# Graph attention sums: ScalarE copies out the bank of the tile that precedes an item's tile, and TensorE works batch by batch

## The reference

```python
q, k, v = h @ Wq, h @ Wk, h @ Wv                     # [n, 8, 32] each
e = sum(q[dst] * k[src], -1) / sqrt(32)              # a score for each edge and head
a = exp(e - segment_max(e, dst)[dst])
z = segment_sum(a, dst)
agg = segment_sum(v[src] * a / (z[dst] + 1e-9), dst) # one row a node
h = layer_norm(agg @ Wo + h)
```

## Time and profile before

| | us |
|---|---|
| median of 3 runs | 6584.65 (6556.1 to 6599.15) |
| the profiled execution | 6544.67 |
| its span in the trace | 6542.9 |

### The profile page before, as it was taken

How to read it: one execution, slowest core, us unless ns; L and a number is a source line. 1 busy time by engine, 2 the same in 40 slices (tenths; PEclk the granted TensorE clock), 3 DMA queues, 4 the chain that set the end, 5 groups by cost and what they waited for, 6 DMA issues and landing times. The chain is left out here.

```text
span 6542.9 us, 104165 instructions
## 1 busy us (share of the span) xinstructions
PE 4595.6 (70%) x23436; PEld 3457.5 (53%) x23437; DVE 3985.9 (61%) x7269; ACT 1997.0 (31%) x4726; POOL 2832.8 (43%) x2898
## 2 busy tenths in 40 slices
PE   0678888888778888888876949655556555348990
PEld 0555555555565666666656949643334433315660
DVE  4667777777576777777656656796444445722332
ACT  0134444444323444444424323320000000313440
POOL 0066666666106666666600010004777776060116
PEclk9999999999889999999888979887777776559995
DMA  5465555555236666665530020002333333022113
GB/s 93 136 189 164 163 163 171 165 164 167 84 109 189 172 169 169 173 169 167 161 103 16 0 94 6 2 29 76 104 104 103 103 105 86 27 90 80 61 56 118
DMA packets 351851, 736.53 MB, mean 113 GB/s; under 512 B 74621, under 2 KB 192897, under 8 KB 351566
## 3 DMA queue, kind: packets, MB, share of 16 engines
q0 software_dynamic: 189824, 588.23, 31.5%
q1 hardware_dynamic: 161870, 146.69, 7.8%
HBM read 634.25 MB, written 100.43 MB: 112 GB/s over the span
## 5 line engine op out<-in xcount | busy, mean ns | idle before, releaser
L967 POOL DMA_INDIRECT rows_a<-kv_scratch,att_idx x848 | 854.6, 1008 | 1096.0 <-issue 563.9
L728 POOL DMA_INDIRECT rows_a<-k_scratch,sage_sum_idx x832 | 799.7, 961 | 855.9 <-issue 850.0
L1027 ACT ACTIVATE attention_rows_b<-ps x1664 | 649.3, 390 | 1366.2 <-PE ps L1120 1237.9
L967 POOL DMA_INDIRECT rows_c<-kv_scratch,att_idx x816 | 877.4, 1075 | 417.9 <-issue 247.1
L1103 PE MATMUL ps<-attention_rows_b,att_work 128*128 x3328 | 925.4, 408 | 72.4 <-issue 60.3
L1435 PE MATMUL ps<-rows_a 128*128 128x258 f32 x1664 | 614.9, 534 | 467.5 <-DMA rows_a<-k_scratch,sage_sum_idx 309.4
L1435 PEld LDWEIGHTS ps<-rows_a 128*128 128x128 f32 x1664 | 421.7, 265 | 660.5 <-DVE sage_rows_b L1413 417.2
L1118 PE MATMUL ps<-rows_a,att_work 128*128 128x264 f32 x1696 | 572.5, 455 | 211.0 <-ACT attention_rows_b L1027 165.0
L1103 PEld LDWEIGHTS ps<-attention_rows_b,att_work 128*128 128x128 f32 x3328 | 608.4, 201 | 184.7 <-issue 92.1
L1413 DVE TENSOR_TENSOR sage_rows_b<-sage_rows_b,ps 128x258 f32 x832 | 353.1, 424 | 566.0 <-PE ps L1435 370.5
L1118 PE MATMUL ps<-rows_c,att_work 128*128 128x264 f32 x1632 | 540.2, 448 | 147.8 <-ACT attention_rows_b L1027 119.1
(11 more groups left out here) (395 smaller groups left out, 9304.4 us busy)
## 6 DMA issues: line engine op xcount, KB each, us to landing
kv_scratch<-rows_c SPq DMA_DIRECT2D x100, 256.0 KB
rows_a<-kv_scratch,att_idx POOLq DMA_INDIRECT x848, 3.7
slot_in<-rows_c SPq DMA_DIRECT2D x1, 13568.0 KB
rows_a<-slot_in SPq DMA_DIRECT2D x106, 128.0 KB
slot_out<-rows_a POOLq DMA_DIRECT2D x106, 128.0 KB
rows_a<-k_scratch,sage_sum_idx POOLq DMA_INDIRECT x832, 2.8
rows_c<-kv_scratch,att_idx POOLq DMA_INDIRECT x816, 3.7
h_scratch<-rows_a SPq DMA_DIRECT2D x2, 6400.0 KB
```

The source lines that it names most:

```text
L728: pool.indirect_dma_start(ring[:, slot, 0:D], None, table, bass.IndirectOffsetOnAxis(ap=idx[:, slot:slot + 1], axis=0)).then_inc(landed[sl ...
L967: pool.indirect_dma_start(r.halves[h][:, u, 0:KV], None, c.kv_dram[:, :], bass.IndirectOffsetOnAxis(ap=idx[:, slot:slot + 1], axis=0)).the ...
L1027: a.activation(c.rows_b[:, bass.ds(at[u], QW)], c.ps[:, bass.ds(in_bank(c, at[BATCH + u]), QW)], ACT.Copy).then_inc(copied, 1)
```

## The change

The table of places gets a fourth kind, and the three kinds of banks are 1: the bank of the *preceding* tile, 2: the bank of the item's tile, 3: the bank of the next tile. `keep` now copies the bank of the preceding tile, at the offset at which it wrote before; so `rows_b` holds the sum of tile t one place further on, at t+1, and one more copy at the end fetches the last tile. The sum, the clear and the copy of an item thus touch three different banks. `summed` is incremented by each item's sum, not by the clear of a pair. A copy waits for the sums of all earlier items; a clear waits for the copies of all earlier items; a sum waits for no copy. `rescale_sums` waits for the block's sums rather than for its copies. TensorE takes the sums of a batch in one piece: in q=0 and q=1 directly after the distances and ahead of the expansions, in q=2 and q=3 after the expansions. ScalarE takes the scores in q=3 ahead of `keep`.

```diff
-        self.places = sb("places", [1, BATCHES * 3 * BATCH], I32)
+        self.places = sb("places", [1, BATCHES * 4 * BATCH], I32)
...
-                    for k in range(2):
+                    for k in range(3):
                         sp.dma_start(c.room_dram[k].rearrange("(c p) -> p c", p=P), bank_i[:, k]).then_inc(written, 16)
-                sp.wait_ge(written, 96)
+                sp.wait_ge(written, 112)
...
-                for k in range(2):
-                    do(v.tensor_copy(places[:, :, 1 + k], bank_rows[:, k, 0:ITEMS].rearrange("p (b u) -> p b u", u=BATCH)))
+                for k, to in enumerate((2, 3, 1)):
+                    do(v.tensor_copy(places[:, :, to], bank_rows[:, k, 0:ITEMS].rearrange("p (b u) -> p b u", u=BATCH)))
...
                 def edge_hot(b, n):
                     a.wait_ge(s_spread, b + 1)
-                    need(a, summed, 2 * b - 2)
+                    need(a, summed, 4 * b - 4)
...
-                def keep(b, between=None):
+                def keep(b):
                     at = places_of(a, c, b, 0, 2)
-                    for half in range(2):
-                        if half and between is not None:
-                            take_scores(between)
-                        a.wait_ge(summed, 2 * b + half + 1)
-                        for u in (2 * half, 2 * half + 1):
-                            need(a, copied, b * BATCH + u)
-                            a.activation(c.rows_b[:, bass.ds(at[u], QW)], c.ps[:, bass.ds(in_bank(c, at[BATCH + u]), QW)],
-                                         ACT.Copy).then_inc(copied, 1)
+                    for u in range(BATCH):
+                        need(a, summed, b * BATCH + u)
+                        need(a, copied, b * BATCH + u)
+                        a.activation(c.rows_b[:, bass.ds(at[u], QW)], c.ps[:, bass.ds(in_bank(c, at[BATCH + u]), QW)],
+                                     ACT.Copy).then_inc(copied, 1)
...
+                        if q == 3 and within(i, ROUND, k + 1, 0, BLOCKS):
+                            take_scores(blk + 1)
                         if sums:
-                            keep(g, blk + 1 if q == 3 and within(i, ROUND, k + 1, 0, BLOCKS) else None)
+                            keep(g)
...
-                a.wait_ge(copied, ITEMS)
+                a.wait_ge(summed, ITEMS)
+                last = 5 * 512 + NODE_TILES % 3 * 512
+                a.activation(c.rows_b[:, NT * QW:(NT + 1) * QW], c.ps[:, last:last + QW], ACT.Copy).then_inc(copied, 1)
+                a.wait_ge(copied, ITEMS + 1)
...
-                def add_up(i, n, at, half):
+                def add_up(i, n):
                     b = i * RB + n
-                    need(pe, copied, b * 4 + 2 * half)
-                    if half == 0:
-                        pe.wait_ge(s_ready, b + 1)
-                        pe.wait_ge(messages, b + 1)
-                        if n % 4 == 0:
-                            need(pe, rescaled, i * 2 * ROUND + n // 4 * 2)
+                    at = places_of(pe, c, b, 2, 2)
+                    pe.wait_ge(s_ready, b + 1)
+                    pe.wait_ge(messages, b + 1)
+                    if n % 4 == 0:
+                        need(pe, rescaled, i * 2 * ROUND + n // 4 * 2)
                     rows = r.batch(n)
-                    for u in (2 * half, 2 * half + 1):
+                    for u in range(BATCH):
                         pe.matmul(c.ps[:, bass.ds(in_bank(c, at[u]), QW)], r.s[n % 2][:, u, :], rows[:, u, D:SLOT],
-                                  start=False, stop=True, skip_group_check=True)
-                        mm = pe.matmul(c.ps[:, bass.ds(in_bank(c, at[BATCH + u]), 1)], c.zeros[:, :], c.zeros[:, 0:1],
-                                       start=True, stop=True)
-                    mm.then_inc(summed, 1)
+                                  start=False, stop=True, skip_group_check=True).then_inc(summed, 1)
+                        need(pe, copied, b * BATCH + u)
+                        pe.matmul(c.ps[:, bass.ds(in_bank(c, at[BATCH + u]), 1)], c.zeros[:, :], c.zeros[:, 0:1],
+                                  start=True, stop=True)
...
-                        if q != 3:
-                            spread(q)
+                        spread(q)
                         if q == 2:
                             turn_weights(blk)
-                        if sums:
-                            at_sum = places_of(pe, c, i * RB + g, 1, 2)
-                        if ahead:
-                            at_q = places_of(pe, c, i * RB + u, 0, 1)
-                        if q == 2 and ahead:
-                            expand(i, u, at_q, 0)
-                            expand(i, u, at_q, 1)
-                        if sums:
-                            add_up(i, g, at_sum, 0)
+                        if q < 2 and sums:
+                            add_up(i, g)
                         if q == 0:
                             turn_ends(blk)
                         if q == 1:
                             carry_columns(blk)
-                        if q == 2:
-                            spread(3)
+                        if ahead:
+                            at_q = places_of(pe, c, i * RB + u, 0, 1)
+                            expand(i, u, at_q, 0)
                         if q == 3 and within(i, ROUND, k + 1, 0, BLOCKS):
                             turn_scores(blk + 1, k + 1)
-                        if q != 2 and ahead:
-                            expand(i, u, at_q, 0)
-                        if sums:
-                            add_up(i, g, at_sum, 1)
-                        if q != 2 and ahead:
+                        if ahead:
                             expand(i, u, at_q, 1)
+                        if q >= 2:
+                            add_up(i, g)
...
                 def rescale_sums(blk):
                     v.wait_ge(r_ready, blk + 1)
-                    v.wait_ge(copied, blk * BLOCK)
-                    at = in_bank(c, places_of(v, c, blk * 4, 1, 1)[0])
+                    v.wait_ge(summed, blk * BLOCK)
+                    at = in_bank(c, places_of(v, c, blk * 4, 2, 1)[0])
```

More of the change, by code:

```diff
@@ L362, in _ @@
                 do(v.tensor_copy(row_f, c.item_tile[:, :]))
-                places = c.places[:, :].rearrange("p (b k u) -> p b k u", k=3, u=BATCH)
+                places = c.places[:, :].rearrange("p (b k u) -> p b k u", k=4, u=BATCH)
                 do(v.tensor_scalar(places[:, :, 0], row_f[:, 0:ITEMS].rearrange("p (b u) -> p b u", u=BATCH),
                                    float(QW), None, ALU.mult))
-                for k in range(2):
-                    do(v.tensor_copy(places[:, :, 1 + k], bank_rows[:, k, 0:ITEMS].rearrange("p (b u) -> p b u", u=BATCH)))
+                for k, to in enumerate((2, 3, 1)):
+                    do(v.tensor_copy(places[:, :, to], bank_rows[:, k, 0:ITEMS].rearrange("p (b u) -> p b u", u=BATCH)))
                 each = row_f.rearrange("p (b u) -> p u b", u=BATCH)
@@ L906, in places_of @@
 def places_of(eng, c, b, first, kinds):
-    at = c.places[0:1, bass.ds(b * 3 * BATCH + first * BATCH, kinds * BATCH)]
+    at = c.places[0:1, bass.ds(b * 4 * BATCH + first * BATCH, kinds * BATCH)]
     return c.nc.values_load_multi_w_load_instructions(
@@ L1002, in stage @@
                 def stage(g, n):
-                    need(a, summed, 4 * g - 20)
+                    need(a, summed, 8 * g - 40)
                     a.activation(idx[:, n * HALF:(n + 1) * HALF], c.src_idx[:, bass.ds(g * HALF, HALF)],
@@ L1535, in norm @@
                 def norm(g, parity):
-                    sums = c.rows_b[:, bass.ds(g * 2 * SUMW, 2 * SUMW)].rearrange("p (t n) -> p t n", t=2)
+                    sums = c.rows_b[:, SUMW:][:, bass.ds(g * 2 * SUMW, 2 * SUMW)].rearrange("p (t n) -> p t n", t=2)
                     v.wait_ge(turned, g + 1)
```

24 lines of the change are left out of this document (11 added, 13 removed).

## The result

| | before | after |
|---|---|---|
| median of the runs, us | 6591.9 (6556.1 to 6609.92, 4 runs) | 6337.07 (6333.12 to 6339.42, 4 runs) |
| profiled execution, us (its span) | 6544.67 (6542.9) | 6339.42 (6337.8) |
| ratio after/before | | 0.9619, 95% interval 0.9577 to 0.9661 |

The changed kernel is 3.8% faster. Between the medians lie 255 us, between the two profiled spans 205.1.

A forecast was written before the change was run, and what follows sets the result against it. TensorE with its waits was taken to set the pace. Blocks 115, loop's turn -6, tables -6, tail +12, last copy -1 made 114, say 115 us, off the 6584.65 median: 6470 us, range 6350 to 6600.

The forecast's parts named there:

- The banks and waits: Mid-loop blocks: pair waits for copies go, new clear waits just covered; 23.7 us for 24.8, 115 us over 104 blocks.
- The stall at the second clear: TensorE in q=0 and again in q=1: second clear waits for ScalarE's first copy, made behind its tables; 0.65 us each.
- The wait for the messages: TensorE in q=2, before the first sum: grows from 0.48 to 1.36 us, where part of the gain goes.
- The tables: Table of places: a third column of bank numbers adds a scattered write on the path; 6 us.
- eight increments more a block: Each sum carries a semaphore increment, 16 a block for 8: nothing counted; 22 us in all if they serialize.
- The layout: The block laid out phase by phase from earlier trace durations: 23.7 us a block, time 6410 to 6520, chance 0.47.
- the baseline: Median of three timed runs, 6584.65 us, 40 above the profiled run; the same 115 us taken from it.
- The tail: Last two batches of a layer: some five uncovered 1.19 us pair waits go; 12 us, less 1 for the last copy.
- The loop's turn: One block in three: ScalarE's lateness stands whole before the second clear, 2.6 us for 2.43; costs 6 us.
- (a): Rival: cover complete, the two stalls and the reads go; block 22.1 to 22.4 us, time 6335; chance 0.14.
- (b): Rival: nothing gained, the wait moves to the softmax chain; block 24.5 to 25 us, time 6555 to 6620; chance 0.21.
- (c): Rival: lockstep, sum-copy-clear round 0.3 us longer, block 1.2 us longer than before, 6720 us; chance 0.14.

The follow-up runs named there:

- fill: Kernel before plus six matmuls that compute nothing, in q=3 where TensorE waited for a copy: 6530.17 us, ratio 0.9895.
- wrap_fill: Changed kernel plus ten matmuls that compute nothing, before the second clear of q=0 in each third block: 6351.41 us, ratio 0.9713.
- tail_fill: Kernel before plus four matmuls that compute nothing behind each half of the sums, in a layer's last block and two batches only: 6577.51 us, ratio 1.0005.
- copy_first: Changed kernel with ScalarE's first copy ahead of its two tables in q=0 and q=1: 6324.5 us, ratio 0.959.
- copy_reads: Changed kernel with ScalarE's first copy ahead of its tables in q=0 and q=1, and TensorE's reads of places moved ahead: 6328.11 us, ratio 0.9675.
- slow_copy: Changed kernel with a small ScalarE operation and a wait for it ahead of each copy: 6725.73 us, ratio 1.0287.

## Why the prediction was right and where it failed

*The banks and waits: right in mechanism and size.* Mid-loop 23.5 us where 23.7 was laid out, 1.23 us a block less and not 1.1. The stall at the second clear of q=1 was 0.68 for 0.65, that of q=0 0.28: the clear came at t=2.17 for 2.28, but the read ahead of the sums had already made TensorE 0.26 late there. The issue gap of 0.62 us went; 0.26 of waiting for the multiply came in its place. The wait for the messages grew to 0.92 and not to 1.36. Reads on the path: 0.17 to 0.32 us for 0.15. `local_max` lost its wait and gathers stayed hidden. The copies behind two waits each follow at 0.58 us and not at the 0.52 taken, so ScalarE is slower than an item and not faster; over the four copies of a batch no clear of q=2 or q=3 came to wait for it. The tables took 3.8 us more for 6 (the first instruction of VectorE behind them, L795, starts at 92.15 us for 88.38), but the first layer's first turn of the scores stands at 373.5 us for 373.8, so nothing of it is left there. Of the eight increments more a block nothing is to be seen: with one on each sum the pace is 0.563 us, as it was. The rule that the prediction named stands in the Trainium skill on the page "TensorE: Matmul & The Clock Gate", section "The cost: per-tile semaphore tail", not on the page that the prediction gave. By it the pace would be 0.576 on the mean of all items, an estimate; the trace does not agree.

*The step that failed is the clock.* The layout counted idle time at its own length, with every matmul at the durations of the earlier trace rows, as if what TensorE is granted were the same before and after. The mean in the earlier trace rows, 25.9 us a block against 24.8, was ascribed to the turn of ScalarE's loop; the second layer, with 25.42 us a block at clock 0.96 and no turn that is 2.5 us late, was not looked at. There a block of before at full clock takes 24.8 or 24.7 us, and 25.3 where the loop turns (2693.13 to 2718.40, the one such block at clock 1.00). The 44 blocks between the first four and the last three took 27 us more than that. After, the same 44 took 0.6 us more than 23.5 and, at the turns, 24.0. The gain of the second layer is 32 us over 51 times 1.23; 26 to 27 of them are this, which no term of the sum held, and the rest lies in the first and last blocks and was not taken apart. `fill`, `wrap_fill` and the trace of `tail_fill` show the clock at work apart from the change. The Trainium skill, "TensorE: Matmul & The Clock Gate", "A second HAM failure mode: psum-queue depth-cycling", tells of a kernel whose short idles between groups of matmuls, from cycling through PSUM banks, make the clock go to and fro between its levels; these traces agree (1.26 us of idle, then 1.24 us for a matmul pair of 0.71).

*The same error in the baseline.* The prediction took the 40 us by which the median of before lay above the profiled run over to the changed kernel. They did not carry over: after, the four runs lie within 6.3 us of each other, and the profiled one is the longest of them. On three chips the median of before was 6600, 6534 and 6548 us, while `copy_first` on the first and its near kin `copy_reads` on the second came within 4 us of each other (6324.5 and 6328.1). That alone is 40 us of the 133 between 6470 and 6337. That they were clock too is inferred: the added work of `fill` took the spread away, and of the 13 runs of before beside it the quickest (6535 us) had the highest granted clock of the whole run, 0.866, the others 0.835 to 0.857, though not in the order of their times.

*The tail was mis-sized,* 11 us for 44.8. The earlier trace rows showed 1.19 us of waiting at the lower clock, and the prediction took five such waits a layer off. But thirteen pairs of sums stand behind the last turn of the scores, as the last block has no expansions either, and with the waits gone the clock rises (0.51 to 0.89), which shortens the matmuls themselves. `tail_fill` gives the share of the clock: 14 us a layer with every wait for a pair of copies left in, 28 of the 44.8. The 16.5 left over are not far from the 11 laid out for the waits.

*The loop's turn was mis-sized, without harm.* The block of 27.23 us in the earlier trace rows was the mildest of the first layer's; they run to 29.9. With mid-loop blocks alone (24.73 and 23.5 us) the first layer's 51 would take 1261.2 us before and 1198.5 after; they took 59.9 and 60.2 more, so the turns cost the same in both and not 6 us more. In the second layer a turn costs 0.5 us at full clock, before (25.3 for 24.8) as after (24.0 for 23.5).

The sum by terms, profiled execution against profiled execution: blocks 157.5 us for 109 predicted (10 of the difference from the pace, 6 from the turns, 32 from the second layer), tails 44.8 for 11, all else 2.8 gained for 6 lost: 205.1 for 114. These 91 us, the baseline's 40 and the 2 by which the profiled run of after lies above its median are the miss of 133.

*The rivals.* (a), complete cover at 6335 us, names nearly the time measured, but not by its mechanism: the block is 23.5 us, not 22.1 to 22.4, and the stalls are there. A right number from a wrong reason would have been believed, had only the time been looked at. (b) occurred in part: the wait for the messages grew by 0.44 us. (c) did not. `slow_copy` brought it about, and its price was too low: (c) spread a round 0.3 us longer over two items and gave 2.4 us a block, while each copy also waits for the one before, so that an item of `slow_copy` takes up to 0.26 us more and its mid-loop block 2.8 to 4.6. That its 6726 us are close to the 6720 of (c) is chance. What stays open is why ScalarE's loop turns 2.4 to 3.3 us late in the first layer and costs 0.5 us in the second, and what decides, at the same idle places, whether an execution of the kernel before keeps its clock for a layer or loses it in each block; no run here separates these.

## What to carry to other kernels

Read the granted clock of every stage and of the tails before summing a stall: where it is under 1.00, the wait costs its length and then the slower matmuls behind it, and a change that closes it gives back both, and the spread between runs with it. Where a change has two parts, price each alone; here the banks brought more than the whole, and the order by batch took some back. An idle engine beside the one that sets the pace (VectorE's 2.33 us) is not yet a bound.

## What the runs showed of the hardware

- TensorE fell to its lower level behind idle places of 0.81 and 1.26 us in blocks of 24.8 us, and not every time: in the second layer of before 12 of 51 blocks kept the full clock (0.96 on the mean of the layer), in that of `tail_fill` 3 did (0.88), 78.4 us apart over 51 blocks of the same program.
- Work that computes nothing made the kernel before 1.05% faster on the median (6530 for 6600 us) and its spread 11 us for 90 (`fill`).
- ScalarE's copies with two waits each follow at 0.58 us, not 0.52, and still no clear of q=2 or q=3 waited for one at an item each 0.563 us; with ScalarE's round at 0.82 us (`slow_copy`) the sums follow at 0.82.
